# FP4 quantising on 16-bit halves in larger parts, node ranks as sums of signs on ScalarE, six chunks' base products ahead of the tail, takes replanned

## The chip, the cores and the metric

The program runs on one core of a Trainium2 chip. The metric is the device time of one execution in microseconds (us), the median of three runs. Engines are named as in the profile: PE is TensorE (matmul; PEld its weight loads), DVE is VectorE, ACT is ScalarE, POOL is GpSimd, SP is SyncE, which issues most DMA transfers. The engines run their own instruction streams in order and wait for each other through semaphores.

## The reference, cut to what matters

1,250 nodes with 1,024 features, 40,000 edges sorted by their receiver. The output is x plus a graph attention layer plus a mixing layer, and then a feed-forward layer in FP4.

```python
xn = _layernorm(x, axis=-1)
x = x + _L0_gnn_ref(xn, edge_index, ...) + _L0_mix_ref(xn[None], ...)[0]
x = x + _L0_ffn_ref(_layernorm(x, axis=-1)[None], gate_w, up_w, down_w, s_in, s_in_down)[0]

# attention: per edge, message, score, softmax over the edges of a receiver, weighted sum
msg = xl[src] + xr[dst]
act = jnp.where(msg > 0, msg, NEG_SLOPE * msg)
e = jnp.einsum('ehd,hd->eh', act, att)
out = jax.ops.segment_sum(alpha[..., None] * xl[src], dst, num_segments=n)

# feed-forward: weights and rows are rounded to FP4 with a scale for each block of 16
amax = jnp.max(jnp.abs(xb), axis=-1, keepdims=True)
sc8 = jnp.clip(amax / FP4_MAX * global_scale, 0.0, FP8_MAX).astype(jnp.float8_e4m3fn)
q = jnp.sign(xb) * _FP4_VALS[jnp.digitize(a, _FP4_MIDS)]      # 0, .5, 1, 1.5, 2, 3, 4, 6
```

## The kernel before, in words

Nodes lie in 10 chunks of 128. The work has three stages.

**The opening.** x is normalised (`xhat`), turned on PE (`xhat_t`) and multiplied by the small attention weights (groups `hid`, `lr`, `lin`); two tables, `xr_table` and `msg_table`, go to HBM. PE then forms the Gram matrix (`gram`, 16 groups). Meanwhile DVE counts the edges of each node (`one_hots`, `hist`), and ranks the nodes by their count, so that nodes with about as many neighbours share a chunk: `key_row` holds all 1,280 keys in every partition, `key_col` the own ones, and for each chunk one `tensor_scalar` compares the row with the own key and sums (`rank_f`). POOL scatters node, start and degree to their place (`perm_dram`), SP reads them back (`placed`, semaphore `perm_in`), POOL reads the neighbour lists (`neigh`) and the `xr` rows, and DVE makes the indices `idx` from which POOL gathers message rows.
DVE also quantises the three feed-forward weights (n = 0 to 2: gate, up, down). `weight_max(n)` takes the largest of each block of 16, `weight_factors(n)` makes the scales, and `piece(q)` rounds a quarter of a weight: `quantized` on 1,024 columns, from `wslot[n % 2]` to `wq_bf[q % 2]`, with `wt` as scratch. SP stores each piece (`store(q)`); they come back turned in the tail. The rounding works on f32 words: a mask keeps the exponent and sets one bit below it, and adding and subtracting that number rounds the value.

**The rounds.** 62 rounds of 5 or 6 neighbours for each of 128 nodes. In round g, DVE multiplies by `att_sb` (L1626), sums over features (L1628), takes the smallest score (L1633), adds the receiver to the next round's rows (`add_receiver`, L1456) and sums the weighted rows of the round before (`close`, L1464). ACT makes the exponentials (L1081) and the weighted rows (L1094), POOL gathers and rescales.
In the same time PE forms the mixing layer's products: groups `p`, `kv`, `t1`, `t2` (16 each), two `bias` groups, and `base`, two for each of the first EARLY chunks: 1,024 x 1,024 products of `xhat_t` and `mat_a`, 128x512 in f32, 8 matmuls a group. Every group goes to the next of four PSUM banks, and DVE or ACT must take group n - 4 before group n starts. In which round a take stands is planned ahead by a few numbers, not by what PE has done: `PRODUCTS_AT`, `ROUND_0_AT`, `ROUND_STEP`. `sum_p0(n)`, 16 in all, sum weight rows times `colsum` on DVE; eight stand ahead of round 0 and eight in rounds 0 to 3.

```python
at = max(at, freed.get(n - 4, 0))
at += GROUP_STEP.get(kind, 7.0)
round_of[n] = max(0, math.ceil((at - ROUND_0_AT) / ROUND_STEP))
```

**The tail.** The attention comes back from HBM (`gnn_dram`), PE turns it (L894) and adds it by two halves a chunk: `x2(c, h)` (L884), with the base products first where c >= EARLY (L881). The order of these is the table `X2_PLAN`. DVE adds each half (`residual`, L1566), `tail_scales(k)` and `rows_rounded` / `hidden_rounded` call `scales` and `quantized` for 1,024 and 512 columns, PE turns the rows (L903), multiplies by the gate and up weights (L914) and by the down weight (L936). DVE, PE and ACT work on neighbouring chunks in a pipeline of steps k.

## Time and profile before

| | |
|---|---|
| median of three runs | 927.51 us |
| lowest and highest | 926.6 and 928.5 us |
| span of the profiled execution, from its first to its last instruction (no other time of it is given) | 926.9 us, 0.6 below the median |
| busy in it: PE | 858.0 us (93%) |
| DVE | 859.4 us (93%) |
| ACT | 551.4 us (59%) |
| POOL | 471.8 us (51%) |

The profile is of one execution of its own, so sums are made in its 926.9 us. A busy share says nothing of where an engine waits; the views below go by stretches of the span, by groups of instructions, and by instructions in order of time with what ended the idle time ahead of them.

### The profile page before, as it was taken

How to read it: one execution, taken by the hardware profiler on the slowest of the kernel's cores; microseconds unless marked ns; L12 is line 12 of the kernel's file. 1: busy time of each engine (PE TensorE's matmuls, PEld its weight loads, DVE VectorE, ACT ScalarE, POOL GpSimd, SP SyncE). 2: the span in 40 equal slices, each digit the busy share in tenths (PEclk: the TensorE clock that was granted, in tenths of full speed). 3: DMA queues.
4: the chain of work that ended last, by engine and by line, in shares of the span. 5: the costliest groups of instructions: out<-in, count | busy, mean ns of one | idle time of the engine just before them, and what ended most of it. 6: DMA issues, size and time to landing. Idle time of an engine off the chain costs nothing.

```text
span 926.9 us, 9510 instructions
## 1 busy us (share of the span) xinstructions
PE 858.0 (93%) x2724; PEld 419.7 (45%) x2734; DVE 859.4 (93%) x988; ACT 551.4 (59%) x1949; POOL 471.8 (51%) x512
## 2 busy tenths in 40 slices
PE   4999999999999999999999999999999679989664
PEld 3885455644444444444444444444444234444221
DVE  6999989969999999999999999999998599999995
ACT  3313123208687887879998988888888333343422
POOL 5200445376677767777777777877872100010101
PEclk9999999999999999999999999999999798999868
DMA  9322635362385333563345633349830311113124
GB/s 304 97 104 42 149 115 174 111 201 70 80 184 187 95 88 94 190 214 93 100 108 183 193 97 100 100 105 250 317 78 16 104 44 45 69 24 68 26 42 86
DMA packets 64946, 109.97 MB, mean 119 GB/s; under 512 B 29223, under 2 KB 36036, under 8 KB 64874
## 3 DMA queue, kind: packets, MB, share of 16 engines
q0 software_dynamic: 19856, 55.42, 24.0%
q1 hardware_dynamic: 45034, 53.92, 18.3%
q8 instruction: 21, 0.34, 0.2%
q14 instruction: 35, 0.29, 0.1%
HBM read 89.15 MB, written 17.17 MB: 115 GB/s over the span
## 4 chain that ended last, share of the span: by engine, by line
DVE 67%; issue 14%; POOL 10%; DMA 3%; PE 3%; ACT 1%; SPq 0%; DVEq 0%; ACTq 0%; POOLq 0%
DVE z L1628 9%; DVE turned L1456 9%; DVE turned L1626 8%; DVE acc_sb L1464 8%; POOL round_mem L551 7%; DVE round_mem L1210 3%; DVE round_mem L1214 2%; DVE round_mem L1211 2%; DVE round_mem L1209 2%; DVE round_mem L1206 2%; DVE round_mem L1207 2%; DVE round_mem L1208 2%; DVE big_b L1418 1%; DVE big_a L1421 1%; DVE big_b L1566 1%
## 5 line engine op out<-in xcount | busy, mean ns | idle before, releaser
L551 POOL DMA_INDIRECT round_mem<-msg_table,idx x352 | 342.8, 974 | 116.8 <-issue 79.4
L1094 ACT ACTIVATE round_mem<-round_mem,pz 128x65 f32<-128x65 f32 x1408 | 354.4, 398 | 6.9 <-DVE acc_sb L1464 3.0
L726 PE MATMUL acc<-wslot,big_a 128*128 128x512 f32 x512 | 222.3, 597 | 3.1 <-DVE big_b L1418 3.1
L726 PEld LDWEIGHTS acc<-wslot,big_a 128*128 128x128 f32 x512 | 97.8, 192 | 126.0 <-issue 123.8
L1464 DVE TENSOR_REDUCE acc_sb<-round_mem 128x260 f32<-128x1820 f32 (+1 forms) x62 | 121.6, 1962 | 6.5 <-ACT round_mem L1094 4.0
L1081 ACT ACTIVATE pz<-z 128x7 f32<-128x7 f32 (+1 forms) x248 | 55.5, 296 | 106.8 <-DVE z L1633 106.4
L726 PE MATMUL acc<-wslot,big_b 128*128 128x512 f32 x256 | 110.0, 593 | 0.0
L726 PE MATMUL acc<-big_b,wslot 128*128 128x512 f32 x256 | 110.0, 593 | 0.0
L1456 DVE TENSOR_TENSOR turned<-round_mem,turned 128x1560 f32<-128x1560 f32 (+1 forms) x62 | 105.4, 1700 | 2.3 <-DVE z L1633 0.2
L1628 DVE TENSOR_REDUCE z<-turned 128x24 f32<-128x1560 f32 (+1 forms) x62 | 105.1, 1695 | 2.1
L1626 DVE SCALAR_TENSOR_TENSOR turned<-turned,att_sb 128x1536 f32<-128x1536 f32 (+1 forms) x62 | 103.6, 1671 | 0.0
L726 PE MATMUL acc<-big_a,xhat_t 128*128 128x512 f32 x224 | 96.3, 593 | 0.0
L726 PE MATMUL acc<-big_b 128*128 128x512 f32 (+3 forms) x240 | 80.7, 496 | 0.0
L726 PEld LDWEIGHTS acc<-wslot,big_b 128*128 128x128 f32 x256 | 48.7, 190 | 61.1 <-issue 61.1
L726 PEld LDWEIGHTS acc<-big_b,wslot 128*128 128x128 f32 x256 | 48.7, 190 | 61.1 <-issue 61.1
L726 PEld LDWEIGHTS acc<-big_a,xhat_t 128*128 128x128 f32 x224 | 42.6, 190 | 53.5 <-issue 53.2
L671 POOL TENSOR_TENSOR round_mem<-acc_sb,pz 128x260 f32<-128x260 f32 x62 | 47.7, 769 | 33.5 <-DVE acc_sb L1464 29.7
L693 POOL TENSOR_TENSOR rstd<-small,minus_half 128x1 f32<-128x1 f32 x10 | 7.2, 718 | 105.3 <-ACT small L1107 105.3
L726 PEld LDWEIGHTS acc<-big_b 128*128 128x128 f32 x240 | 43.1, 194 | 35.2 <-issue 29.5
L1160 ACT ACTIVATE round_mem<-acc,cscale 128x512 f32<-128x512 f32 x10 | 6.9, 687 | 66.7 <-PE acc L914 66.7
L699 POOL DMA_DIRECT2D out_x<-acc_sb x9 | 8.0, 890 | 72.9 <-ACT acc_sb L1117 69.2
L1024 ACT COPY big_a<-acc 128x512 f32<-128x512 f32 x16 | 9.2, 587 | 58.1 <-PE acc L726 42.6
(222 smaller groups left out, 1043.5 us busy)
## 6 DMA issues: line engine op xcount, KB each, us to landing
big_b<-in_x SPq DMA_DIRECT2D x18, 512.0 KB, 10.4
round_mem<-msg_table,idx POOLq DMA_INDIRECT x352, 2.8
out_x<-big_b SPq DMA_DIRECT2D x9, 512.0 KB, 2.6
out_x<-acc_sb POOLq DMA_DIRECT2D x9, 512.0 KB, 5.5
wslot<-in_wv_t SPq DMA_DIRECT2D x2, 2048.0 KB, 11.5
wslot<-in_wk_t SPq DMA_DIRECT2D x2, 2048.0 KB, 12.5
wslot<-in_wo_t SPq DMA_DIRECT2D x2, 2048.0 KB, 10.0
wslot<-in_wq SPq DMA_DIRECT2D x2, 2048.0 KB, 10.1
```

Of the source, the lines that this page charges most:

```text
L551: pool.indirect_dma_start(xg[g % 4][:, j, :], None, msg_table, bass.IndirectOffsetOnAxis(idx[:, c, j0 + j:j0 + j + 1], 0)).then_inc(xg_in[ ...
L671: nc.gpsimd.tensor_tensor(halves_of[g % 3][:, :, :, n].rearrange("p i (h d) -> p i h d", d=MR), running[c].rearrange("p (i h d) -> p i h d ...
L726: mm = nc.tensor.matmul(o(acc[:, n % 4, :]), a, b, start=first, stop=last)
L1081: ins = nc.scalar.activation(pz[:, g % 2, 0:slots + 1, h], z[:, g % 3, 0:slots + 1, h], ACT.Exp, scale=-1.0, bias=z[:, (g + 1) % 3, top_sl ...
L1094: ins = nc.scalar.activation(to[:, :, j], xg[g % 4][:, j, h * HR + 1:(h + 1) * HR], ACT.Copy, scale=pz[:, g % 2, j, h:h + 1])
L1206: step(nc.vector.tensor_tensor(blocks(v), blocks(v), spread(inv), ALU.mult))
L1207: step(nc.vector.tensor_scalar(t.bitcast(I32), v.bitcast(I32), EXPONENT, HALF_BIT, ALU.bitwise_and, ALU.bitwise_or))
L1210: step(nc.vector.scalar_tensor_tensor(to, v, 6.0 * UP + FP4_MAX, t, ALU.min, ALU.subtract))
L1456: return nc.vector.tensor_tensor(m4[:, 0:n], xg[g % 4][:, 0:n, :].rearrange("p j (h d) -> p j h d", d=HR)[:, :, :, 0:MR], receiver.unsquee ...
L1464: nc.vector.tensor_reduce(running[c].rearrange("p (i f) -> p i f", i=2), halves_of[g % 3][:, :, :, 0:n + 1], AX.X, ALU.add).then_inc(sum_d ...
L1626: step(nc.vector.scalar_tensor_tensor(m4[:, 0:slots, :, 1:MR], m4[:, 0:slots, :, 1:MR], 0.0, att_sb[0:NC].unsqueeze(1).to_broadcast([NC, s ...
L1628: step(nc.vector.tensor_reduce(zz[:, 0:slots, :], m4[:, 0:slots], AX.X, ALU.add))
```

## The change

- `quantized` works on 2,048 columns of a weight at a time (six pieces in place of twelve), and, after the multiply by `inv` in f32, on 16-bit values: a mask takes the upper half of each f32 word and lays the elements of a row out turned (first all first elements of the blocks, then all second ones), and seven further steps are `tensor_scalar` and `tensor_tensor` on bf16. The block scale `sc8` is bf16. The rounded values are written over the slot's own memory (`steps_of`), so the next weight's load into the slot waits for their stores as well (`wt_out`).
- The ranks are made on ACT: the sum of the signs of the differences, one `activation` for each chunk, between and behind the takes of `lr`; DVE turns the sums into ranks (`rank_i`).
- DVE's order in the opening changes with it: the ranks are waited for behind `weight_factors(1)`, ahead of piece 2; only piece 2 stands between them and the wait for `placed`, and pieces 4 and 5 stand behind the indices.
- All 16 `sum_p0` stand in rounds 0 to 7.
- EARLY is 6: chunk 6's base products are made in the tail, in `x2(6, h)`. `ROUND_0_AT` is 168, `X_AT` 55: takes and `add_bias` stand in other rounds.

```diff
-EARLY = 7
+EARLY = 6
...
-HALF_BIT = 0x00400000
-UP = 2.0 ** 22
+CELL, MIDDLE = 0xFFE0, 0x0010
+BINADE, HALF_BIT = 0x7F80, 0x0040
...
-ROUND_0_AT, ROUND_STEP = 196.0, 8.5
+ROUND_0_AT, ROUND_STEP = 168.0, 8.5
 
...
-BIAS_SUMS_AT, X_AT = 40, 54
+BIAS_SUMS_AT, X_AT = 40, 55
...
+        cells = wt.bitcast(BF16)
+        steps_of = [wslot[q // 2 % 2][:, q % 2 * 2 * D:q % 2 * 2 * D + D].bitcast(BF16) for q in range(6)]
...
+                to = gu_dram[q * 2 * P:(q + 1) * 2 * P, :] if q < 4 else dn_dram[(q - 4) * 4 * P:(q - 3) * 4 * P, :]
+                j = 2 if q < 4 else 4
+                sp.dma_start(to.rearrange("(j p) d -> p j d", p=P),
+                             steps_of[q].rearrange("p (j d) -> p j d", j=j)).then_inc(wt_out[q // 2], 16)
...
             sp.wait_ge(w_quantized, 1)
+            sp.wait_ge(wt_out[0], 32)
             sp.dma_start(view(2), uses[2][1]).then_inc(w_in[0], 16)
...
+            def rank(c):
+
+                if c == 0:
+                    act.wait_ge(key_in, 32)
+                nc.scalar.activation(is_above, key_row, ACT.Sign, scale=-1.0, bias=key_col[:, c:c + 1],
+                                     accum_out=rank_f[:, c:c + 1]).then_inc(ranked, 1)
+                act.wait_ge(ranked, c + 1)
+
             for c in range(C):
                 take(index_of["lr", c])
+                if c >= 4:
+                    rank(c - 4)
+            for c in range(6, C):
+                rank(c)
             take(index_of["lin", 0])
...
-                step(nc.vector.tensor_tensor(sc8, sc8, magic, ALU.subtract))
+                step(nc.vector.tensor_tensor(amax, amax, magic, ALU.add))
+                step(nc.vector.tensor_tensor(sc8, amax, magic, ALU.subtract))
...
-                step(nc.vector.tensor_tensor(blocks(v), blocks(v), spread(inv), ALU.mult))
-                step(nc.vector.tensor_scalar(t.bitcast(I32), v.bitcast(I32), EXPONENT, HALF_BIT, ALU.bitwise_and, ALU.bitwise_or))
-                step(nc.vector.tensor_scalar(t, t, 1.5 * UP, 6.0 * UP, ALU.max, ALU.min))
-                step(nc.vector.scalar_tensor_tensor(v, v, 1.0 / UP, t, ALU.mult, ALU.add))
-                step(nc.vector.scalar_tensor_tensor(to, v, 6.0 * UP + FP4_MAX, t, ALU.min, ALU.subtract))
-                return nc.vector.scalar_tensor_tensor(blocks(to), blocks(to), -FP4_MAX, spread(sc8), ALU.max, ALU.mult)
+                nb = width // QB
+                rows_in = v.shape[1] // width
+
+                def turned_blocks(a):
+                    return a.rearrange("p (r i b) -> p r i b", r=rows_in, i=QB)
+
+                high = v.bitcast(U16).rearrange("p (r b i t) -> p r i b t", r=rows_in, i=QB, t=2)[:, :, :, :, 1]
+                by_block = v.rearrange("p (b i) -> p b i", i=QB)
+                step(nc.vector.tensor_tensor(by_block, by_block, inv.unsqueeze(2).to_broadcast([v.shape[0], rows_in * nb, QB]), ALU.mult))
+                step(nc.vector.tensor_scalar(turned_blocks(cell.bitcast(U16)), high, CELL, MIDDLE, ALU.bitwise_and, ALU.bitwise_or))
+                step(nc.vector.tensor_scalar(way.bitcast(U16), cell.bitcast(U16), BINADE, HALF_BIT, ALU.bitwise_and, ALU.bitwise_or))
+                step(nc.vector.tensor_scalar(way, way, 1.5, 64.0, ALU.max, ALU.mult))
+                step(nc.vector.tensor_tensor(cell, cell, way, ALU.add))
+                step(nc.vector.tensor_tensor(way, cell, way, ALU.subtract))
+                step(nc.vector.tensor_scalar(way, way, -FP4_MAX, FP4_MAX, ALU.max, ALU.min))
+                spread = sc8.rearrange("p (r b) -> p r b", r=rows_in).unsqueeze(2).to_broadcast([v.shape[0], rows_in, QB, nb])
+                return nc.vector.tensor_tensor(turned_blocks(to), turned_blocks(way), spread, ALU.mult)
...
-                n, i = divmod(q, 4)
+                n, i = divmod(q, 2)
                 if q >= 1:
                     dve.wait_ge(wq_done, q)
-                if q >= 2:
-                    dve.wait_ge(wt_out[q % 2], 16 * (q // 2))
-                sc8, inv = (f[:, i * 64:(i + 1) * 64] for f in w_factors[n][0:2])
-                quantized(wslot[n % 2][:, i * D:(i + 1) * D], wq_bf[q % 2], (sc8, inv), wt).then_inc(wq_done, 1)
+                inv, sc8 = (f[:, i * 128:(i + 1) * 128] for f in w_factors[n][0:2])
+                quantized(wslot[n % 2][:, i * 2 * D:(i + 1) * 2 * D], steps_of[q], (sc8, inv), cells, steps_of[q],
+                          D if n < 2 else I).then_inc(wq_done, 1)
...
-            piece(0)
             dve.wait_ge(hist_read, PIECES)
             step(nc.vector.tensor_copy(hist, hist_ps))
             step(nc.vector.tensor_tensor_scan(hist_inc, ones32, hist, 0.0, ALU.mult, ALU.add))
             nc.vector.tensor_copy(tot[:], hist_inc[:, DG_LO - 1:DG_LO]).then_inc(tot_done, 1)
             step(nc.vector.tensor_scalar(key, hist, DEG_MAX, KEY_STEP, ALU.min, ALU.mult))
             nc.vector.tensor_tensor(key, key, key_node, ALU.add).then_inc(key_done, 1)
-            piece(1)
+            piece(0)
             step(nc.vector.tensor_tensor(hist_exc, hist_inc, hist, ALU.subtract))
             dve.wait_ge(off_done, 1)
             nc.vector.tensor_scalar(hist_exc, hist_exc, tp[0:DG_HI, 1, 0:1], None, ALU.add).then_inc(csr_done, 1)
             weight_max(1)
-            dve.wait_ge(key_in, 32)
-            for c in range(C):
-                step(nc.vector.tensor_scalar(is_above, key_row, key_col[:, c:c + 1], None, ALU.is_gt, ALU.add,
-                                             accum_out=rank_f[:, c:c + 1]))
-            nc.vector.tensor_copy(rank_i, rank_f).then_inc(rank_done, 1)
-            piece(2)
-            piece(3)
+            piece(1)
             weight_end(0)
             weight_factors(1)
-            piece(4)
+            dve.wait_ge(ranked, C)
+            nc.vector.tensor_scalar(rank_i, rank_f, -0.5, 0.5 * (NP - 1), ALU.mult, ALU.add).then_inc(rank_done, 1)
+            piece(2)
...
-            piece(5)
...
-            piece(6)
-            piece(7)
+            piece(3)
             weight_end(1)
...
-            weight_factors(2)
-            piece(8)
...
-            piece(9)
-            piece(10)
-            piece(11)
+            weight_factors(2)
+            piece(4)
+            piece(5)
             weight_end(2)
...
-            for n in range(KB):
-                sum_p0(n)
...
-                if g < KB // 2:
-                    sum_p0(KB + 2 * g)
-                    sum_p0(KB + 2 * g + 1)
+                if g < KB:
+                    sum_p0(2 * g)
+                    sum_p0(2 * g + 1)
...
-            add_bias(C - 2)
+            for c in range(min(LAST + 1 - X_AT, C - 2), C - 1):
+                add_bias(c)
```

DVE in the opening, between the largest of the second weight and the nodes' flags. Before, from the ranks on (two pieces, factors and a third piece follow them, each piece the six instructions L1206 to L1211):

```order
L1334 TENSOR_SCALAR round_mem<-round_mem 128x1280 [waits key_in]
L1334 TENSOR_SCALAR round_mem<-round_mem 128x1280 [waits dve_step] x9
L1336 CAST round_mem<-round_mem 128x10 [waits dve_step]
L1206 TENSOR_TENSOR wslot<-wslot,round_mem 128x1024 [waits wt_out0,wq_done]
L1207 TENSOR_SCALAR round_mem<-wslot 128x1024 [waits dve_step]
```

Of the changed kernel, from the end of `weight_factors(1)` to the wait for `placed`:

```order
L1347 TENSOR_SCALAR round_mem<-round_mem 128x10 [waits ranked,dve_step]
L1216 TENSOR_TENSOR wslot<-wslot,round_mem 128x2048 [waits wq_done]
L1217 TENSOR_SCALAR round_mem<-wslot 128x2048 [waits dve_step]
L1218 TENSOR_SCALAR wslot<-round_mem 128x2048 [waits dve_step]
L1219 TENSOR_SCALAR wslot<-wslot 128x2048 [waits dve_step]
L1220 TENSOR_TENSOR round_mem<-round_mem,wslot 128x2048 [waits dve_step]
L1221 TENSOR_TENSOR wslot<-round_mem,wslot 128x2048 [waits dve_step]
L1222 TENSOR_SCALAR wslot<-wslot 128x2048 [waits dve_step]
L1224 TENSOR_TENSOR wslot<-wslot,round_mem 128x2048 [waits dve_step]
L1350 TENSOR_TENSOR round_mem<-placed,cap_f 128x10 [waits perm_in]
```

The ten compares are gone from DVE, the wait for ACT's sums (`ranked`) stands there, and one piece is left ahead of the wait for `perm_in`.

DVE at the first round. Before (`big_b` at L1584 and L1587 is the sum of `sum_p0`, L1418 is the take of a `p` group):

```order
L1584 TENSOR_SCALAR big_b<-wslot,colsum 128x512 [waits w_in1,colsum_done,acc_full]
L1587 SCALAR_TENSOR_TENSOR big_b<-wslot,colsum,big_b 128x512 [waits p0_summed] x7
L1454 COPY turned<-xr_sb 128x260 [waits xr_in]
L1456 TENSOR_TENSOR turned<-round_mem,turned 128x1560 [waits xg_in0,dve_step]
L1418 SCALAR_TENSOR_TENSOR big_b<-big_b,colsum,acc 128x512 [waits vb_in,acc_full,dve_step]
L1418 SCALAR_TENSOR_TENSOR big_b<-big_b,colsum,acc 128x512 [waits vb_in,acc_full] x2
L1626 SCALAR_TENSOR_TENSOR turned<-turned,att_sb 128x24x64
```

Of the changed kernel:

```order
L1454 COPY turned<-xr_sb 128x260 [waits xr_in]
L1456 TENSOR_TENSOR turned<-round_mem,turned 128x1560 [waits xg_in0,dve_step]
L1624 SCALAR_TENSOR_TENSOR turned<-turned,att_sb 128x24x64 [waits dve_step]
L1626 TENSOR_REDUCE z<-turned 128x24 [waits dve_step]
L1630 COPY z<-top_first 128x4 [waits dve_step]
L1631 TENSOR_REDUCE z<-z 128x4 [waits dve_step]
L1456 TENSOR_TENSOR turned<-round_mem,turned 128x1560 [waits xg_in1,z_done]
L1584 TENSOR_SCALAR big_b<-wslot,colsum 128x512 [waits colsum_done,w_in1,acc_full,dve_step]
L1587 SCALAR_TENSOR_TENSOR big_b<-wslot,colsum,big_b 128x512 [waits p0_summed]
```

Eight sums and three takes stood ahead of round 0's first product; now they stand two by two in the rounds, and the first take in round 2.

PE in the tail, from the fourth turning of attention to the first turned rows. Before:

```order
L894 MATMUL turned<-ident,acc_sb 128x128 x4
L884 MATMUL acc<-wslot,xr_sb 128x512 x4
L884 MATMUL turned<-wslot,xr_sb 128x512 x2
L894 MATMUL turned<-ident,acc_sb 128x128 x4
L884 MATMUL turned<-wslot,xr_sb 128x512 x4
L903 MATMUL turned<-identb,round_mem 128x128 x8
```

Of the changed kernel:

```order
L893 MATMUL turned<-ident,acc_sb 128x128 x4
L883 MATMUL acc<-wslot,xr_sb 128x512 x4
L880 MATMUL turned<-big_a,xhat_t 128x512 x8
L883 MATMUL turned<-wslot,xr_sb 128x512 x2
L893 MATMUL turned<-ident,acc_sb 128x128 x4
L883 MATMUL turned<-wslot,xr_sb 128x512 x4
L902 MATMUL turned<-identb,round_mem 128x128 x8
```

The eight base products (L880) of `x2(6, 1)` stand ahead of the last two chunks' attention and of the first turned rows; those of `x2(6, 0)` stand two steps later in the same way.

## Rows read from the trace of the kernel before

**Rows 1.** Windows: us, busy us (instructions) per engine, PE clock, DMA share, GB/s

```profile
60.60:187.20 126.60, 126.60 (x459) 72.59 (x456) 117.79 (x149) 34.06 (x90) 43.54 (x42) 0.97 0.45 128
...
204.30:721.00 516.70, 512.68 (x1203) 227.93 (x1201) 501.82 (x414) 429.85 (x1702) 377.21 (x403) 1.00 0.48 133
721.00:927.00 206.00, 154.99 (x546) 70.03 (x556) 178.25 (x313) 69.26 (x120) 16.96 (x20) 0.88 0.23 56
```

**Rows 2.** Timeline of DVE, one piece: start, duration, instruction, count

```profile
55.43 0.16 DVE L1285 RECIPROCAL cscale<-gmax 128x1 f32<-128x1 f32 x1
...
60.60 1.23 DVE L1206 TENSOR_TENSOR wslot<-wslot,round_mem 128x1024 f32<-128x1024 f32 x1
...
66.98 0.17 DVE L1322 COPY round_mem<-turned 40x32 f32<-40x32 f32 x1
```

**Rows 3.** DVE's groups by shape: count, busy us and mean ns, idle before

```profile
L1211 DVE SCALAR_TENSOR_TENSOR round_mem<-round_mem 128x1024 bf16<-128x1024 bf16 x18 | 22.0, 1225 | 0.6
L1334 DVE TENSOR_SCALAR_CACHE_REDUCE round_mem<-round_mem 128x1280 bf16<-128x1280 f32 x10 | 15.4, 1545 | 0.3
...
L1206 DVE TENSOR_TENSOR round_mem<-round_mem 128x1024 f32<-128x1024 f32 x10 | 12.2, 1225 | 0.3
...
L1207 DVE TENSOR_SCALAR round_mem<-round_mem 128x1024 int32<-128x1024 int32 x10 | 7.0, 697 | 0.3
...
L1206 DVE TENSOR_TENSOR round_mem<-round_mem 128x512 f32<-128x512 f32 x10 | 6.9, 686 | 0.1
...
L1261 DVE TENSOR_TENSOR wslot<-round_mem 125x3200 bf16<-125x3200 bf16 x2 | 3.6, 1820 | 0.0
```

**Rows 4.** ACT's groups by shape

```profile
L1105 ACT ACTIVATE round_mem<-big_b,mean_var 128x1024 bf16<-128x1024 f32 x10 | 11.5, 1148 | 0.3
```

**Rows 5.** Timeline of ACT, first half of the take of lr 4

```profile
77.84 0.47 ACT L1009 ACTIVATE acc_sb<-acc,rrms 128x256 f32<-128x256 f32 x1 [0.88 <-PE acc L726]
```

**Rows 6.** Timeline of POOL in the opening

```profile
95.69 1.90 POOL L600 DMA_INDIRECT perm_dram<-round_mem  x1 [15.84 <-DVE round_mem L1336]
...
126.61 1.03 POOL L629 DMA_INDIRECT round_mem<-src_table,start_i  x1 [1.89 <-issue]
...
153.47 0.94 POOL L633 DMA_INDIRECT xr_sb<-xr_table,node_pi  x1 [0.30 <-issue]
```

**Rows 7.** Timeline of SP's queue

```profile
108.81 1.22 SPq L484 DMA_DIRECT2D wslot<-in_down_w  x1
118.54 0.36 SPq L487 DMA_DIRECT2D placed<-perm_dram  x1
```

**Rows 8.** Timeline of DVE, its waits in the opening and round 0

```profile
123.56 0.17 DVE L1343 TENSOR_TENSOR round_mem<-placed,cap_f 128x10 f32<-128x10 f32 x1 [3.21 <-DMA placed<-perm_dram]
...
194.16 0.49 DVE L1584 TENSOR_SCALAR big_b<-wslot,colsum 128x512 f32<-128x512 f32 x1 [6.96 <-issue]
...
204.34 1.76 DVE L1626 SCALAR_TENSOR_TENSOR turned<-turned,att_sb 128x1536 f32<-128x1536 f32 x1
```

**Rows 9.** Timeline of PE, base products and first work of the tail

```profile
622.79 96.30 PE L726 MATMUL acc<-big_a,xhat_t 128*128 128x512 f32 x224
728.15 1.11 PE L894 MATMUL turned<-ident,acc_sb 128*128 128x128 f32 x4 [9.07 <-DMA acc_sb<-gnn_dram]
```

**Rows 10.** Timeline of ACT, exponentials of round 54

```profile
654.45 0.88 ACT L1081 ACTIVATE pz<-z 128x6 f32<-128x6 f32 x4
```

**Rows 11.** Windows of the tail

```profile
728.15:783.15 55.00, 47.53 (x139) 21.68 (x142) 44.66 (x82) 18.83 (x39) 1.73 (x3) 0.88 0.14 55
783.15:864.41 81.26, 74.66 (x269) 33.99 (x272) 77.74 (x134) 31.37 (x55) 7.71 (x9) 0.98 0.21 52
```

**Rows 12.** Timeline of DVE in the tail: chunk 6's second half, one hidden chunk

```profile
785.45 0.69 DVE L1566 SCALAR_TENSOR_TENSOR big_b<-acc,big_b 128x512 f32<-128x512 f32 x1
...
848.62 0.69 DVE L1206 TENSOR_TENSOR round_mem<-round_mem 128x512 f32<-128x512 f32 x1
...
852.33 0.74 DVE L1535 SCALAR_TENSOR_TENSOR round_mem<-acc,cscale,round_mem 128x512 f32<-128x512 f32 x1
```

More of the change, by code:

```diff
@@ L229, in gps_layer @@
         key_done = sem("key_done")
-        rank_done, perm_out, perm_in = sem("rank_done"), sem("perm_out"), sem("perm_in")
+        ranked, rank_done = sem("ranked"), sem("rank_done")
+        perm_out, perm_in = sem("perm_out"), sem("perm_in")
         xr_out, xr_in = sem("xr_out"), sem("xr_in")
@@ L237, in gps_layer @@
         tail_w_in = sem("tail_w_in")
-        wt_out = [sem("wt_out0"), sem("wt_out1")]
+        wt_out = [sem(f"wt_out{n}") for n in range(3)]
         stored = sem("stored")
@@ L291, in gps_layer @@
         qa = tail_mem[0:NC, 3 * D:4 * D]
+        row_cells, row_steps = (qa[:, i * I:(i + 1) * I].bitcast(BF16) for i in range(2))
         x_last = tail_mem[0:LAST_ROWS, 3 * D:4 * D]
@@ L305, in gps_layer @@
         tail_max, tail_g = blocks_of[:, 0], blocks_of[:, 1]
[L306 removed]
+        tail_factors = [(blocks_of[:, 4 + 2 * i, 0:NB // 2].bitcast(BF16), blocks_of[:, 5 + 2 * i]) for i in range(2)]
         gnn_out = [xr_sb[:, c, 0:HID] for c in range(C)]
@@ L471, in _ @@
                 sp.dma_start(unplaced[:, :, 2], csr_dram[1].rearrange("(c p) -> p c", p=NC)).then_inc(csr_in, 16)
-            store(1)
+            store(0)
             sp.wait_ge(csr_done, 1)
@@ L477, in _ @@
                 sp.dma_start(unplaced[:, :, 1], csr_dram[0].rearrange("(c p) -> p c", p=NC)).then_inc(csr_in, 16)
-            store(2)
             sp.wait_ge(acc_taken["act"], taken[index_of["lin", 0]])
@@ L481, in _ @@
             sp.dma_start(msg_table.rearrange("(c p) f -> p c f", p=NC), acc_sb[:]).then_inc(table_out, 16)
-            store(3)
+            store(1)
             sp.wait_ge(w_quantized, 1)
+            sp.wait_ge(wt_out[0], 32)
             sp.dma_start(view(2), uses[2][1]).then_inc(w_in[0], 16)
@@ L487, in _ @@
                 sp.dma_start(placed[:], perm_dram.rearrange("(c p) t -> p c t", p=NC)).then_inc(perm_in, 16)
-            for q in range(4, 8):
+            for q in range(2, 4):
                 store(q)
             sp.wait_ge(w_quantized, 2)
+            sp.wait_ge(wt_out[1], 32)
             sp.dma_start(view(3), uses[3][1]).then_inc(w_in[1], 16)
-            for q in range(8, 11):
-                store(q)
+            store(4)
             sp.wait_ge(acc_full, index_of["gram", 15] + 1)
@@ L496, in _ @@
             sp.dma_start(bk_bc, bk.rearrange("(a d) -> a d", a=1).to_broadcast([P, D])).then_inc(vb_in, 16)
-            store(11)
+            store(5)
             sp.wait_ge(w_quantized, 3)
+            sp.wait_ge(wt_out[2], 32)
             sp.dma_start(view(4), uses[4][1]).then_inc(w_in[0], 16)
@@ L508, in _ @@
             sp.wait_ge(acc_full, read_by[10])
-            sp.wait_ge(wt_out[0], 16 * 6)
-            sp.wait_ge(wt_out[1], 16 * 6)
+            for n in range(3):
+                sp.wait_ge(wt_out[n], 32)
             for k in range(4):
@@ L1192, in scales @@
                 if g.shape[1] == 1:
[L1193 to L1211 removed]
+                    return nc.vector.tensor_scalar(inv, magic, g, TIE_UP, ALU.mult, ALU.mult)
@@ new lines, in scales, with quantized @@
+                return nc.vector.scalar_tensor_tensor(inv, magic, TIE_UP, g, ALU.mult, ALU.mult)
+            def quantized(v, to, factors, cell, way, width):
+                sc8, inv = factors
+                nb = width // QB
[13 more added lines that the diff above has]
+                return nc.vector.tensor_tensor(turned_blocks(to), turned_blocks(way), spread, ALU.mult)
@@ L1557, in hidden_rounded @@
                 sc8, inv = tail_factors[(c + 1) % 2]
-                quantized(hidden, h_bf[c % 2], (sc8[:, D // QB:], inv[:, D // QB:]), qa[:, 0:I]).then_inc(h_done, 1)
+                quantized(hidden, h_bf[c % 2], (sc8[:, D // QB:], inv[:, D // QB:]), row_cells[:, 0:I], row_steps[:, 0:I], I).then_inc(h_done, 1)
             def residual(c, h):
@@ L1601, in add_base @@
                 step(nc.vector.tensor_tensor(b, base_at[c], b, ALU.add))
-            assert round_of[index_of["bias", 1]] < X_AT <= LAST - (C - 3)
+            assert round_of[index_of["bias", 1]] < X_AT
             def sum_bias(k):
```

50 lines of the change are left out of this document (13 added, 37 removed).

## The prediction

> **What bounds the kernel now.** First the busy shares by stage, then who waits in each. In the opening (60.6 to 187.2) VectorE (DVE) is busy 117.8 of 126.6 us and TensorE (PE) all of it; in the 62 rounds DVE is busy 501.8 and PE 512.7 of 516.7 us; in the tail DVE 178.3 and PE 155.0 of 206 us [rows 1]. PE is not waited for in the rounds: it runs the products ahead of DVE and must only be done when the tail starts. It ends the base products at 622.79 + 96.30 = 719.1 and then stands idle 9.1 us for the attention that comes back from HBM at 728.2 [rows 9]. So DVE's order of work sets the start of the rounds and their end, and PE is some 9 us short of being the bound there. In the opening DVE waits only twice, 3.2 us for the sorted nodes (`placed`) at 123.6 and 7.0 us at 194.2, behind the branch over the skipped overflow block [rows 8]. The first product of round 0 (the multiply by `att`) starts at 204.34.
>
> **One piece.** A piece is six instructions on 1,024 columns, 60.60 to 66.98, 6.4 us [rows 2], so 12.8 for 2,048. The new one has eight on 2,048. The rows give the rates: two-source f32 686 ns for 512 columns and 1,225 for 1,024, so 0.15 + 1.05 ns per element; two-source all in 16 bits 1,820 ns for 3,200, so 0.15 + 0.52; one-source 32-bit, the int32 mask included, 697 for 1,024, so 0.15 + 0.52; `scalar_tensor_tensor` gains nothing from bf16, 1,225 for 1,024 [rows 3]. Then:
> - the f32 multiply by `inv`: 2.29 us.
> - the three `tensor_tensor` in bf16: 0.15 + 2,048 x 0.52 = 1.22 each, 3.66.
> - the three one-source operations in 16 bits: no row has one. Above they cost the 32-bit row's 1.22 each. Two bytes in place of four double the two-source rate [rows 3]; the same factor gives 0.15 + 2,048 x 0.26 = 0.69. I take 0.69, 2.07 for three. The Trainium skill, VectorE: DVE Perf Modes, section The perf-mode tier table, gives 693 ns for such an operation on 2,048 bf16 elements; by it the sum stays as it is, and no run here shows it yet.
> - the mask that reads the upper halves, 64 bytes apart, and writes them turned: no row has such a stride. Its nearest rows are the same mask on neighbouring words, 0.52 ns an element (1.22), and the two-source f32 row, 1.05 (2.29). I take the middle, 1.76: the stride may cost the rate that the mask has now, or nothing, and no row tells.
>
> Sum 9.78, and 0.2 for the gaps of 0.03 to 0.04 between dependent instructions: **10.0 us**, bounds 9.4 to 12.1. Six pieces: 60 us in place of 77.
>
> **The opening.** The ten compares of the ranks leave DVE, 15.4 us [rows 3], 16 with reading each sum. On ScalarE (ACT) one costs 1.15 us for 1,024 elements with an accumulator [rows 4], so with a quarter more elements and the reading of the sum about 1.5. Six of them sit behind the takes of lr 4 to 9, each 0.85 us [rows 5]: from 78.7 on ACT goes 2.35 per chunk, to 91.9, and four more end at **97.9**. PE is not held: it has four banks, and its next groups (`lin` and the first gram groups) need only lr 6 to 9 taken, done by 90.6 while PE is still at the first of them. DVE meanwhile: it starts the ranks now at 95.3 - 16 = 79.3, with two pieces behind it. Without these 12.8 us, with pieces 0 and 1 (20.0), the factors of the second weight that now stand ahead of the wait (5.2 by 55.43 to 60.60 [rows 2], and 0.3 to end the first) and 1.2 because the histogram has no piece in front of it any more, it comes there at 93.2 and waits 4.7 us. The ranks are done 2.6 us later than now, so the ten scatters on GpSimd (POOL) start at 98.3 and not 95.7 and end at 112 [rows 6].
> Their data took until 118.5 to be seen by SyncE, beside the 2-MB weight load issued at 108.8, and `placed` landed at 123.5 [rows 7, 8]. Now that load waits for the store of piece 1, which queues behind the two table writes, to about 115; the scatters thus meet less traffic. I set this against the 2.6 us: `placed` at **124**, 119 to 130. Behind this wait stand on DVE the starts of all neighbour lists, and POOL's neighbour reads (126.6 now) wait for them. DVE has only piece 2 to do ahead of it (done at 108.1), so 15 us of the saving turn into a longer wait.
> From the wait to 187.2 DVE now needs 63.6 us with seven pieces (44.8), so 18.8 of other work. After: 124 + 18.8 + 3 x 10.0 + 0.6 for the third weight, that lands about 126 = **173.4**. POOL is no later: its neighbour and xr reads run 126.6 to 154.4 [rows 6] and keep their distance to `placed`; the first gather can then start at 155, and all lists are ready before that. Then the 7.0 us behind the branch stay. Of the 17.1 us from 187.2 to 204.34 the first eight column sums (5.9) and three takes (2.1) go into the rounds, 9.2 stay: round 0's first product at 182.6, **21.7 earlier**.
>
> **The rounds.** The 5.9 and 2.1 come back inside them, and one `add_bias` of 1.2 moves behind them: 21.7 - 5.9 - 2.1 + 1.2 = **14.9 earlier** at their end; the attention is back at 728.2 - 14.9 = 713.3. PE: two base groups of 96.30 / 14 = 6.9 us are gone, 705 if nothing held it. But takes stand in later rounds (the last t2 take in round 54, was 51). PE can be four groups ahead of them; it starts the second base group when round 54's take is done, near 654.4 - 13.7 = 640.7 [rows 10], and 11 groups end at 716.4. That is 3 us behind the attention, paid for by the first tail products, which come at full clock and not after a gap of 9 us (granted clock 0.88 in that stretch, against 0.98 after) [rows 11]. I count 0.
>
> **The tail.** PE gets chunk 6's base products, 2 x 6.9 = 13.8 us, the first half ahead of the first turned rows. In its first 55 us PE is busy 47.5 [rows 11]: with 13.8 more it needs 61.3, some 4 less at full clock (0.88 is granted now). Of its 7.5 idle us there I let it fill 2 (the rest are waits for ACT and DVE at fixed places): chunk 6's second half is ready 13.8 - 4 - 2 = 7.8 later. PE has it now at 783.1, DVE adds it at 785.4 [rows 12], 2.3 later: so DVE stands 5.5 us later from there. After that DVE is the longer of the two, 77.7 of 81.3 us busy against PE's 74.7. A row chunk (1,024) saves by the same rates 6.38 - 5.7 = 0.7, a hidden chunk (512) 848.62 to 852.33 = 3.7 - 3.55 = 0.15 [rows 12]: 0.85 in each of 7 to 8 steps, 6.4 in all. Added base and bias sums even out. Tail: 5.5 - 6.4 = **-0.9**, near nothing.
>
> Sum: 14.9 + 0.9 = 15.8 off the span of 926.9, rounded down to 15.5 for the steps where PE is as long: 911.4. The median of the runs is 0.6 above that span: **912.0 us**, 1.7% faster.
>
> **Rivals.**
> - *The strided mask is slow (slower).* Its place: piece 3 to 5 and each tail chunk. If each element cost two cycles (2.08 ns, twice the one-a-cycle row) a piece grows by 2.65, the three by 8, a tail step by 2.0, nine of them by 18: 938 us. It decides from 0.78 + 0.76 = about 1.55 ns an element. For it: nothing in the trace reads with such a stride. Against it: the int32 mask has two elements a cycle to give away. Chance 0.12. A rule of the Trainium skill speaks for it: Vector Engine (DVE) Microarchitecture Reference, section 5.2 Measured stream behaviour, says a stream that hops at every element takes 1.7 to 2.5 ns per element in place of 1.05. At 2.5 ns the same sum gives 948; no run here shows it.
> - *The 16-bit one-source operations run like the 32-bit ones.* A piece is 11.6, a tail step 1.2 longer: 4.8 + 10 on top, 927, no change. Chance 0.06.
> - *The chain of the ranks or PE takes the gain.* `placed` at 130 and not 124 puts all 6 us onto the start; or PE's 13.8 us in the tail are not absorbed. 918 to 925. For it: DVE waits there already; PE is busy 99% of the rounds. Chance 0.17.
> - *More than that.* The mask at two a cycle (0.5 us per piece and tail chunk, 3 to 4 us in all) and a shorter stop behind the branch, which now coincides with a 2-MB load: 900 to 906. Chance 0.2.
>
> The forecast's own case, 906 to 918, has 0.45. Within 0.2% (1.9 us, about what three runs can tell from no change) lie the second rival and edges of the first and third, 0.05; slower 0.13; faster 0.82. Range 902 to 926.
>
> **What would show it.** Right: eight instructions a piece, 9.4 to 10.5 us; a wait of 12 to 18 us at `perm_in`; the `att` product of round 0 near 183; rounds ending about 15 us earlier; PE's idle gap ahead of the tail gone; the tail as long as now, with DVE waiting for PE around chunk 6. Wrong: a mask above 3 us for 2,048; takes that wait in the rounds for PE; `placed` later than 130; a tail longer by more than 5 us.

## The result and the profile after

The changed kernel took 937.8 us (median; 935.1 to 942.2), the kernel before 927.1 beside it: ratio 1.0122, 95% interval 1.0101 to 1.0144. The forecast was 912.0. The profiled execution has a span of 935.0 us, clock 0.968. One execution in this document is left out of the ratios: 5,109 us, one of the ten of e10.

VectorE's groups in the opening (out<-in, shapes, count | busy us, mean ns of one | idle before):

```profile
L1217 DVE TENSOR_SCALAR round_mem<-wslot 128x2048 uint16<-128x2048 uint16 x6 | 11.8, 1968 | 0.2
L1216 DVE TENSOR_TENSOR wslot<-wslot,round_mem 128x2048 f32<-128x2048 f32 x4 | 9.2, 2296 | 0.0
...
L1220 DVE TENSOR_TENSOR round_mem<-round_mem,wslot 128x2048 bf16<-128x2048 bf16 x6 | 7.3, 1225 | 0.2
...
L1218 DVE TENSOR_SCALAR wslot<-round_mem 128x2048 uint16<-128x2048 uint16 x6 | 4.2, 694 | 0.2
```

The costs of a piece came close to the forecast: 2.30 + 1.97 + 3 x 0.69 + 3 x 1.22 = 10.0 us busy for 2,048 columns, where 9.78 was forecast; with the gaps between its eight instructions piece 3 lasts 10.3 us (132.42 to 142.72), where 10.0 was forecast. So the slowdown is not in the quantising. VectorE's timeline of the opening (start, duration, engine line op, [idle before it <- what ended it]):

```profile
97.61 0.17 DVE L1347 TENSOR_SCALAR round_mem<-round_mem 128x10 int32<-128x10 f32 x1 [3.39 <-ACT round_mem L1057]
...
125.57 0.17 DVE L1350 TENSOR_TENSOR round_mem<-placed,cap_f 128x10 f32<-128x10 f32 x1 [17.66 <-DMA placed<-perm_dram]
...
182.99 0.43 DVE L1454 COPY turned<-xr_sb 128x260 f32<-128x260 f32 x1 [5.41 <-issue]
...
185.28 1.76 DVE L1624 SCALAR_TENSOR_TENSOR turned<-turned,att_sb 128x1536 f32<-128x1536 f32 x1
...
192.88 1.79 DVE L1456 TENSOR_TENSOR turned<-round_mem,turned 128x1560 f32<-128x1560 f32 x1 [3.32 <-DMA round_mem<-msg_table,idx]
```

These answer to [rows 8]. Round 0 starts at 185.28, 19.1 us earlier than before. Then the lead melts. The start of the multiply by `att` (L1626 before, L1624 after), read from the two timelines round by round:

| round | before | after | lead | what took it |
|---|---|---|---|---|
| 0 | 204.34 | 185.28 | 19.1 | |
| 1 | 212.06 | 195.89 | 16.2 | 3.3 waited for gather(1) |
| 4 | 242.65 | 225.76 | 16.9 | |
| 8 | 276.46 | 266.51 | 10.0 | the column sums, now in the rounds to 7 |
| 28 | 442.58 | 435.04 | 7.5 | takes that stood earlier before |
| 41 | 541.11 | 536.88 | 4.2 | 3.5 waited for the last t1 take |
| 55 | 658.25 | 652.79 | 5.5 | |
| 56 | 666.75 | 670.34 | -3.6 | 9.0 waited for x |

Two lines of VectorE's timeline stand behind the last two losses, and two of SyncE's queue behind the second:

```profile
536.21 0.75 DVE L1610 TENSOR_SCALAR big_b<-big_b,bq_col 128x1024 f32<-128x1024 f32 x1 [3.54 <-ACT big_b L1026]
...
669.20 1.23 DVE L1594 TENSOR_TENSOR big_b<-big_b 128x1024 f32<-128x1024 f32 x1 [8.96 <-DMA big_b<-in_x]
```

```profile
644.53 14.41 SPq L516 DMA_TRANSPOSE wslot<-gu_dram  x8
658.99 0.58 SPq L517 DMA_DIRECT2D wslot<-in_w_up  x1
659.61 4.96 SPq L520 DMA_DIRECT2D big_b<-in_x  x9
```

x is loaded behind twelve transposed weight loads, and these wait for the end of t2 on TensorE: 638.8 now, 621.3 before. Why was TensorE 17.6 us late with a VectorE that was early? Its timeline:

```profile
205.86 8.80 PE L725 MATMUL acc<-wslot,big_a 128*128 128x512 f32 x16 [3.15 <-DVE big_b L1421]
...
265.98 20.87 PE L725 MATMUL acc<-wslot,big_a 128*128 128x512 f32 x48 [2.84 <-DVE big_b L1421]
292.18 17.01 PE L725 MATMUL acc<-wslot,big_a 128*128 128x512 f32 x32 [3.65 <-DVE big_b L1421]
...
689.49 21.05 PE L725 MATMUL acc<-big_a,xhat_t 128*128 128x512 f32 x43 [6.24 <-ACT xhat_t L1030]
```

Six such waits for takes, 14.4 us in all, lie between 205 and 292 (before: two, 3.1 us). The windows of 180 to 300, before and then after (columns as in [rows 1]):

```profile
180.00:300.00 120.00, 116.86 (x280) 52.45 (x279) 110.55 (x105) 70.17 (x284) 82.57 (x86) 0.99 0.54 146
```

```profile
180.00:300.00 120.00, 105.58 (x240) 46.09 (x239) 111.29 (x96) 79.26 (x321) 88.58 (x94) 0.94 0.50 130
```

40 products fewer were done by 300: at 96.30 / 224 = 0.43 us each [rows 9] that is 17.2 us (an estimate, but the end of t2 is late by the same 17.6). 11.3 of them are the busy time that is missing; the rest fits the granted clock, 0.94 and not 0.99.

The tail: the first transpose of the attention starts at 733.13 (728.15 before), right behind the last base product and 10.65 us behind the last round's closing sum (9.26 before). From there to the end are 201.9 us (198.75). Windows from 733.1, answering to [rows 11]:

```profile
733.10:788.10 55.00, 49.96 (x155) 23.20 (x156) 41.09 (x86) 19.44 (x41) 1.73 (x3) 0.97 0.12 46
788.10:869.40 81.30, 76.64 (x269) 34.94 (x273) 70.89 (x148) 30.69 (x53) 6.11 (x8) 1.00 0.21 52
```

TensorE and VectorE have changed places: 76.6 busy against 70.9, before 74.7 against 77.7.

### The profile page after: what moved, and what is told of

It is laid out like the page before. It is cut to its first block, busy times and chain, and to the rows that moved or that the text cites. A ratio compares the mean times of both kernels' runs of the same rounds, so it can differ in the third digit from the quotient of the medians.

```text
span 935.0 us, 9515 instructions
## 1 busy us (share of the span) xinstructions
PE 862.1 (92%) x2724; PEld 420.4 (45%) x2734; DVE 820.0 (88%) x983; ACT 564.0 (60%) x1967; POOL 485.4 (52%) x512
## 4 chain that ended last, share of the span: by engine, by line
PE 57%; DVE 21%; issue 7%; POOL 6%; DMA 3%; SPq 2%; ACT 2%; ACTq 0%; POOLq 0%; DVEq 0%
PE acc L725 46%; PE turned L880 2%; DVE turned L1456 2%; DVE z L1626 2%; DVE acc_sb L1464 2%; DVE turned L1624 2%; POOL round_mem L553 2%; SPq L516 2%; PE acc L880 1%; PE acc L883 1%; PE acc L913 1%; POOL round_mem L631 1%; POOL perm_dram L602 1%; DMA big_b<-in_x 1%; PE turned L935 1%
## 5 line engine op out<-in xcount | busy, mean ns | idle before, releaser
L725 PE MATMUL acc<-wslot,big_a 128*128 128x512 f32 x512 | 228.0, 607 | 14.4 <-DVE big_b L1421 14.4
L1626 DVE TENSOR_REDUCE z<-turned 128x24 f32<-128x1560 f32 (+1 forms) x62 | 105.1, 1695 | 2.1
L1624 DVE SCALAR_TENSOR_TENSOR turned<-turned,att_sb 128x1536 f32<-128x1536 f32 (+1 forms) x62 | 103.5, 1670 | 0.0
L725 PE MATMUL acc<-big_a,xhat_t 128*128 128x512 f32 x192 | 85.4, 606 | 7.5 <-ACT xhat_t L1030 6.2
L725 PEld LDWEIGHTS acc<-big_a,xhat_t 128*128 128x128 f32 x192 | 37.3, 195 | 55.5 <-issue 46.1
L698 POOL DMA_DIRECT2D out_x<-acc_sb x9 | 8.3, 926 | 72.0 <-ACT acc_sb L1125 67.4
## 6 DMA issues: line engine op xcount, KB each, us to landing
wslot<-in_wq SPq DMA_DIRECT2D x2, 2048.0 KB, 10.1
```

The lines of the kernel that those rows point to most:

```text
L725: mm = nc.tensor.matmul(o(acc[:, n % 4, :]), a, b, start=first, stop=last)
L1624: step(nc.vector.scalar_tensor_tensor(m4[:, 0:slots, :, 1:MR], m4[:, 0:slots, :, 1:MR], 0.0, att_sb[0:NC].unsqueeze(1).to_broadcast([NC, s ...
L1626: step(nc.vector.tensor_reduce(zz[:, 0:slots, :], m4[:, 0:slots], AX.X, ALU.add))
```

## The experiments

Theory A: the planner puts round 0 at 168, and it is really at 185; takes come 17 us too late for TensorE's four banks, its lateness makes x late, and that stops VectorE. Theory B: VectorE's own added work in the rounds is the cost.

**e1, the plan.**

```diff
-ROUND_0_AT, ROUND_STEP = 168.0, 8.5
+ROUND_0_AT, ROUND_STEP = 180.0, 8.5
```

> The changed kernel with one number altered, ROUND_0_AT = 180 in place of 168, so that the planner's round 0 stands 5 us ahead of where it was measured (185.3) and not 17. Theory A (the takes are planned too late for the products): TensorE's waits for the bias-adding takes in 180 to 300 fall from 14.4 us to under 4, the granted clock there is back at 0.98 or more, the products of t2 end near 622 and not 638.8, the loads of x are issued near 644 and not 659.6, and VectorE's wait of 9.0 us for them shrinks to under 3: 919 to 926 us. Theory B (the column sums and takes that moved into the rounds cost VectorE the time, TensorE only follows): the waits may go, but the rounds end where they did, 724.5, and the time stays within 2 us of 937.

926.5 us, ratio to the kernel before 0.9999 (0.9983 to 1.0016): one number gives back the whole loss, so theory B, which had the time within 2 us of 937, falls. The wait of 3.5 at 536 is gone, the transposed loads go out at 628.0 and not 638.8. But not all waits went. TensorE's timeline:

```profile
265.03 7.13 PE L725 MATMUL acc<-wslot,big_a 128*128 128x512 f32 x16 [1.62 <-DVE big_b L1421]
...
282.54 7.66 PE L725 MATMUL acc<-wslot,big_a 128*128 128x512 f32 x13 [7.01 <-DVE big_b L1421]
```

With one of 1.45 between these two they sum to 10.1 us, so the expected "under 4 us" was missed, and with it the clock (0.96, expected 0.98 or more), the end of t2 (629.5, expected 622) and the wait for x (5.3, expected under 3). The cause: rounds 1 to 8 last 10 us, with two column sums each, and the planner counts 8.5. Round 10 stands in the plan at 180 + 85 = 265 and is at 283.1, 18 us late; before it was 294.3 against 281, 13 late, and in the changed kernel 284.0 against 253, 31 late. The waits for takes follow in the same order: 3.1 us with 13, 10.1 with 18, 14.4 with 31. VectorE still waits 5.28 us for x.

**e2, the order on SyncE.**

```diff
-            (the twelve transposed loads and w_up)
             sp.wait_ge(acc_full, index_of["bias", 1] + 1)
             for c in range(C - 1):
                 sp.dma_start(base[:, c, :], x[c * NC:(c + 1) * NC, :]).then_inc(x_in[c], 16)
+            (the twelve transposed loads and w_up)
```

> The changed kernel with the nine loads of x issued ahead of the twelve transposed weight loads on SyncE and not behind them; the plan of takes stays late. Theory A: the products are as late as before (t2 ends at 638.8), but x lands near 650 and not 669, so VectorE's wait of 9.0 us and TensorE's of 6.2 us behind it go; the rounds end near 715.5; TensorE's last base product ends near 723, the tail starts there: 924 to 929 us. Theory C (the transposed loads are what matters, and become late for the tail): a new wait in the tail, no gain, 935 us or more.

928.1 us, 1.0002 (0.9987 to 1.0016). The plan is still late, TensorE's waits for takes up to 292 are nearly the same (13.2 us), the loads of x go out at 640.15 in place of 659.61, and the 9.0 us on VectorE and the 6.2 on TensorE are gone; the tail starts at 724.1, 9.0 earlier. Theory C falls: the transposed loads are issued from 645 to 683, in the changed kernel from 639 to 659, and the tail is as long (202.2 us against 201.9).

**e3, both.**

> Both edits: ROUND_0_AT = 180 and the loads of x ahead of the transposed weights. Theory A: both causes gone, the rounds end 9 to 15 us earlier than 724.5 and the attention decides the tail's start again, 716 to 723; 914 to 922 us. Theory B: not under 930 us.

921.0 us, 0.9940 (0.9924 to 0.9957), as expected of theory A. TensorE's row ahead of the tail shows that the attention sets the start again, at 717.1:

```profile
717.14 0.66 PE L893 MATMUL turned<-ident,acc_sb 128*128 128x128 f32 x4 [3.80 <-DMA acc_sb<-gnn_dram]
```

**e4, what the strided mask costs.** Six masks in VectorE's wait at `placed`, in the order of the expectation:

```diff
+            step(nc.vector.tensor_scalar(out_of, hop, CELL, MIDDLE, ALU.bitwise_and, ALU.bitwise_or))
+            step(nc.vector.tensor_scalar(po, pu[:, 0:2 * D], CELL, MIDDLE, ALU.bitwise_and, ALU.bitwise_or))
+            step(nc.vector.tensor_scalar(po, near, CELL, MIDDLE, ALU.bitwise_and, ALU.bitwise_or))
...
```

> The changed kernel with six more masks of 2,048 or 1,024 elements on VectorE behind piece 2, where it waits 17.7 us for the sorted nodes; their results are not used. In their order: the upper halves 64 bytes apart, turned, as the kernel has it (1.97 us expected again); 16-bit neighbours (0.69); the upper halves of neighbouring words, 4 bytes apart (1.22 if a 16-bit element in every 32-bit word runs like a 32-bit one; 1.97 if the packing of halves alone costs the time); 16-bit elements 32 bytes apart (1.97 if any far hop costs 0.89 ns; 0.69 if only the read width counts); 1,024 words 64 bytes apart (0.69 at the neighbouring word's rate, 1.06 at 0.89 ns per hop); 1,024 neighbouring words (0.69). The time of the whole stays within 3 us of the changed kernel's.

```profile
107.50 1.97 DVE L1359 TENSOR_SCALAR round_mem<-wslot 128x2048 uint16<-128x2048 uint16 x1
109.51 0.69 DVE L1360 TENSOR_SCALAR round_mem<-wslot 128x2048 uint16<-128x2048 uint16 x1
110.24 1.23 DVE L1361 TENSOR_SCALAR round_mem<-wslot 128x2048 uint16<-128x2048 uint16 x1
111.50 2.05 DVE L1362 TENSOR_SCALAR round_mem<-wslot 128x2048 uint16<-128x2048 uint16 x1
113.58 1.04 DVE L1363 TENSOR_SCALAR round_mem<-wslot 128x1024 int32<-128x1024 int32 x1
114.65 0.69 DVE L1364 TENSOR_SCALAR round_mem<-wslot 128x1024 int32<-128x1024 int32 x1
```

Less 0.15 us to start: neighbours in 16 bits 0.26 ns an element, every second half (4 bytes apart) 0.53, neighbouring words 0.53, any far hop 0.87 to 0.93, for 16-bit elements 32 or 64 bytes apart and for words alike. What costs is the hop, not the width of the element. All three far hops read in the turned order and write neighbours, so hop and turned order are one thing here. The time stayed at 939.0 us in one run: six masks (7.9 us) in a wait cost nothing that one run can show.

**e5, the plan again**: e3 with ROUND_0_AT = 186.

> As the run with both edits, but ROUND_0_AT = 186. With 180 TensorE still waited 9.8 us for takes between 265 and 284, because rounds 1 to 8, which now hold the column sums, last 10 us and not the planner's 8.5. Theory A: those waits fall under 4 us and the last base product ends 6 us or more earlier; the attention (717.1) already set the tail's start, so TensorE's wait ahead of the tail grows from 3.8 to about 9 and the time stays, 919 to 923 us. Against it: if TensorE's lateness still counted somewhere in the rounds, under 918 us.

923.6 us, 0.9965 (0.9949 to 0.9981), just above the expected 919 to 923. TensorE's waits shrink to 2.9 us at 273, it is done with the base products 12.3 us ahead of the attention, and nothing comes of it:

```profile
715.77 1.11 PE L893 MATMUL turned<-ident,acc_sb 128*128 128x128 f32 x4 [12.29 <-DMA acc_sb<-gnn_dram]
```

The tail starts 1.4 us earlier than in e3 and lasts 1.9 longer, 203.1 against 201.3: after the idle 12.3 us its first 55 us run at a granted clock of 0.88 (0.94 in e3 behind 3.8 us, 0.97 in the changed kernel, which has no such gap).

**e6, chunk 6 back ahead of the tail**: e5 with

```diff
-EARLY = 6
+EARLY = 7
```

> The run with ROUND_0_AT = 186 and the loads of x first, and EARLY = 7: chunk 6's base products (13.8 us of TensorE) are back ahead of the tail. Theory: with the takes on time TensorE has some 9 us to spare ahead of the tail, so the tail starts at most 5 us later, and the tail is the old one less VectorE's savings: chunk 6's step stands 5 us earlier in it. Tail 196 to 199 us in place of 201.3; 916 to 921 us. Rival: the 13.8 us are paid in full ahead of the tail, 923 to 926.

912.0 us, 0.9848 (0.9818 to 0.9879), better than the expected 916 to 921 and clear of e5's interval. The idle 12.3 us are filled, the tail starts at 719.5, 3.7 later, and lasts 188.6 us, 14.5 shorter. Windows of its first stretches:

```profile
719.50:774.50 55.00, 48.50 (x160) 22.59 (x163) 48.13 (x100) 22.41 (x45) 2.33 (x4) 1.00 0.17 65
774.50:855.80 81.30, 70.64 (x266) 32.07 (x270) 76.82 (x160) 31.60 (x54) 7.42 (x9) 0.97 0.24 52
```

VectorE is the longer one again, clock 1.00 from the start.

**e7, the ranks back on VectorE**: e5 with the ten compares ahead of piece 1.

```diff
+            dve.wait_ge(key_in, 32)
+            for c in range(C):
+                step(nc.vector.tensor_scalar(is_above, key_row, key_col[:, c:c + 1], None, ALU.is_gt, ALU.add,
+                                             accum_out=rank_f[:, c:c + 1]))
+            nc.vector.tensor_copy(rank_i, rank_f).then_inc(rank_done, 1)
             piece(1)
```

> The run with ROUND_0_AT = 186 and the loads of x first, with the ten compares of the ranks back on VectorE ahead of piece 1. Theory D: VectorE waits 3.4 and 17.7 us ahead of the sorted nodes, so 16 us of compares fit there; the ranks are done at 95.3 and not 97.5, the nodes are back 0 to 2 us earlier, and the time is the same or up to 2 us shorter. Rival (as the prediction counted them): the compares' time comes off VectorE's path, so that they cost 5 us or more.

923.9 us, 0.9972 (0.9955 to 0.9989); e5 has 923.6. Theory D stands: 16 us of VectorE's work taken away or put back make no difference to the time. (In the two profiled executions e7's tail starts 3.6 us later and is 1.6 us shorter.) Its timeline:

```profile
122.06 0.17 DVE L1341 TENSOR_TENSOR round_mem<-placed,cap_f 128x10 f32<-128x10 f32 x1 [1.58 <-DMA placed<-perm_dram]
...
191.30 1.79 DVE L1447 TENSOR_TENSOR turned<-round_mem,turned 128x1560 f32<-128x1560 f32 x1 [4.06 <-DMA round_mem<-msg_table,idx]
```

`placed` is 2.5 us earlier than in e5 (124.6), yet round 1 still waits for gather(1) to 191.3 (190.8): GpSimd starts that gather behind its branch, in which it stands 7.2 us (7.7 in e5).

**e8, column sums in the wait for gather(1)**: e5 with

```diff
+                if g == 0:
+                    for n in range(4):
+                        sum_p0(n)
                 if g < LAST:
                     step(add_receiver(g + 1))
...
-                if g < KB:
-                    sum_p0(2 * g)
-                    sum_p0(2 * g + 1)
+                if 1 <= g < KB - 1:
+                    sum_p0(2 * g + 2)
+                    sum_p0(2 * g + 3)
```

> The run with ROUND_0_AT = 186 and the loads of x first, with four of the sixteen column sums in round 0 ahead of the wait for gather(1) and two in each of rounds 1 to 6. Theory: VectorE waits about 3 us there for GpSimd's gather, and 3.0 us of sums fit into that wait: round 7 starts 2 to 3 us earlier, and so does the tail; 2 to 3 us faster than that run. Rival: the sums' own inputs are not there yet, no gain.

920.7 us, 0.9932 (0.9908 to 0.9955), about 3 us under e5, but the intervals overlap and the profiled tail starts at 716.6, no earlier than e5's. The wait for gather(1) is gone; that this is the gain is not shown.

**e9, EARLY = 7 alone in the changed kernel** (the edit of e6, nothing else).

> The changed kernel with EARLY = 7 and nothing else; the takes stay planned for 168 and x behind the transposed loads. Theory: TensorE is the late one ahead of the tail there (its last base product ends at 733.1, the attention is back near 731.8), so the 13.8 us of chunk 6 push the tail's start to 745 to 747; the tail itself is the 188.6 us of the run with EARLY = 7; 933 to 937 us, no better than the changed kernel's 937.8. Rival (the number of early chunks alone made the change slow): 925 to 928 us.

942.0 us, 1.0159 (1.0125 to 1.0194). The theory had 933 to 937 and a start of the tail at 745 to 747; its direction is right, its size too small, and the rival (925 to 928) falls: x comes another 2.4 us later (11.4 waited), the tail starts at 749.7 behind TensorE and lasts 189.2. VectorE stands at its start:

```profile
753.53 0.69 DVE L1566 SCALAR_TENSOR_TENSOR big_b<-turned,big_b 128x512 f32<-128x512 f32 x1 [17.29 <-PE turned L883]
```

With a late plan chunk 6 is paid ahead of the tail, with fewer early chunks inside it.

**e10, EARLY = 8 in the kernel before.**

> The kernel before with EARLY = 8 and nothing else: chunk 7's base products too stand ahead of the tail, in the 9.1 us that TensorE waits there. Theory E (in the first third of the tail TensorE is what is waited for, and the idle time ahead of it costs clock): the tail starts near 733, 4.8 us later than at 728.15, and is 8 to 13 us shorter than 198.8: 919 to 924 us. Rival (VectorE is the longer of the two in the tail, 77.7 of 81.3 us busy, as the prediction read it): the tail keeps at least 195 us, 927 to 932 us.

931.2 us, 1.0044 (1.0027 to 1.0060). Theory E falls here, the rival is right: the tail starts at 731.2 and lasts 196.8, only 1.9 less. In the old tail VectorE is the longer one (76.9 busy of 81 us from 786, TensorE 67.4), and products taken off TensorE bring little. The filled gap is seen at its front: the first scaling of a hidden chunk (L1535) stands 37.9 us behind the tail's start, 41.1 before; but the nine steps from there to the last take 140.1 us, 138.8 before. So the 188.6 of e6 are not the filled gap alone.

**e11, all together**: e8's sums, with EARLY = 7.

> ROUND_0_AT = 186, the loads of x first, EARLY = 7, and four column sums in round 0 ahead of the wait for gather(1). With EARLY = 7 TensorE works without a gap from 284 to the tail and its last base product ends where the attention is back (719.5), so the sums' 2 to 3 us are hidden behind TensorE: 910 to 912.5 us. Rival: they come off as in the run with EARLY = 6, 908 to 909.5.

909.3 us, 0.9810 (0.9777 to 0.9842), the fastest, 1.9% under the kernel before. The tail starts at 717.1 and lasts 189.7. The rival is nearer (908 to 909.5; the theory had 910 to 912.5): in the profile the tail starts 2.5 us earlier than e6's, so TensorE was not so tight that this could not come through. The intervals of e6 and e11 overlap, so the 2.7 us between their medians are not shown to be real.

## Why the prediction was wrong

**One piece: right.** 10.0 us forecast with its gaps, 10.3 measured. The mask took 1.97 and not 1.76, the f32 multiply 2.30, the one-source operations 0.694. Behind the mask there are six steps on 16 bits, not seven as the text ahead of the prediction has it; the sum has six. The Trainium skill, VectorE: DVE Perf Modes, section The perf-mode tier table, has 693 ns for the one-source operation, and the trace agrees. The 1.7 to 2.5 ns of the Trainium skill, Vector Engine (DVE) Microarchitecture Reference, section 5.2 Measured stream behaviour, stand there in rows of two-source operations on 32-bit words; the one-source mask here took 0.89 ns an element, so the prediction leaned on another case. The strided mask, the slower rival, was priced at 938, which is near the measured time, but that is chance and not the mechanism: it took 0.2 us a piece more than counted. (At 2.5 ns its sum gives 946 and not 948.)

**The opening: right within 2.7 us.** Ranks done at 97.6 (97.9), `placed` at 125.6 (124), a wait of 17.7 (about 16), round 0 at 185.3 (182.6). Two things were missing from it: a wait of 3.7 us for the neighbour lists, and gather(1). "POOL is no later" failed: its first gather starts at 161.2 and not at 155, its branch ends at 180.3, and VectorE gets gather(1) at 192.9, so 2.9 us of the lead go at once. And e7 shows that the ranks' move saves nothing: they leave an engine that waits for their result.

**The rounds: wrong, and this is the step.** "PE is not waited for in the rounds: it [...] must only be done when the tail starts" failed. TensorE was itself made to wait for takes (14.4 us), t2 ended 17.6 us later, x with it, and VectorE waited 9.0 us for x; so the last round starts 3.6 us later than before, where the forecast had it 14.9 earlier. The forecast moved the last round 14.9 us forward by VectorE's sum alone, and said of TensorE "705 if nothing held it", then looked only at the last takes. It never set the planned times against the measured rounds at the first ones. The plan has round 0 at 168, my own forecast 182.6; with rounds that the moved sums stretch to 10 us the takes are 31 us behind the plan at round 10, where they were 13. The first take stands at 205.0; before, three stood at 202.4. So the takes hardly moved at all, though VectorE did. Of the 18.5 us between forecast and measured end of the rounds, 9.0 are the wait for x, which falls to 5.3 with the plan (e1) and goes with the order of the loads (e2), 3.5 the wait for the last t1 take, which goes with the plan (e1), 2.9 gather(1), 2.7 the later start, the rest the sums and takes, about 8.4 in place of 8.0. The sums themselves were priced well; theory B falls with e1. With both edits (e3) the last round starts at 697.3, 10.9 us earlier than before, and the time is 9.0 us above the forecast.

The link over SyncE was not seen either: x waits for t2's end and then behind some 20 us of transposed loads.

**The tail: the shape right, one size wrong.** Forecast +5.5 for chunk 6 and -6.4 for the savings, -0.9 in all; measured +3.1. The ten scalings of hidden chunks (L1535) stand, counted from the tail's start, at 41.1, 57.9 and so on to 179.8 before, at 42.2, 62.9 and so on to 181.1 now. They are 5.0 us later from the second on, near the 5.5 of the forecast; ahead of it VectorE waits for chunk 6's second half.

```profile
795.45 0.69 DVE L1566 SCALAR_TENSOR_TENSOR big_b<-acc,big_b 128x512 f32<-128x512 f32 x1 [4.53 <-PE acc L883]
...
926.86 1.28 DVE L1571 SCALAR_TENSOR_TENSOR big_b<-turned,cscale,big_b 128x1024 f32<-128x1024 f32 x1 [5.11 <-PE turned L935]
```

Up to the last scaling VectorE regains 3.7 and not 6.4, as TensorE with 76.6 of 81.3 us leaves it little room, and behind it 1.8 go again, as the last wait for TensorE grows from 3.1 to 5.1: 5.0 - 3.7 + 1.8 = 3.1. In e6 and in e9, where chunk 6's products are out of the tail, the nine steps from the first to the last scaling take 132.4 us, against 138.8 before: the savings are there, 6.4 us (6.4 forecast).

What was sized wrong is the net of chunk 6. Taken out of the changed kernel's tail it shortens it by 12.7 of its 13.8 us (e9; 14.5 from e5 to e6), and 5.5 were counted. The prediction set "4 of clock" and "2 idle" against it, which were room in the old tail. But TensorE busy up to the tail has a gain of its own: in e9 and e10, without a gap and with chunk 6 ahead, the first scaling stands 37.9 us behind the tail's start and not 41.1. So 12.7 - 3.1 - 6.4 = 3.2, where 3.1 are measured from the kernel before to the changed one. In the old kernel the same 3.2 us at the front came through as 1.9 only (e10).

So the change carries two gains, an earlier start and a cheaper tail step, and was spoilt by numbers beside them: the planned start of the rounds, the order of the loads of x, and one early chunk too few. Not settled: how much of e8's 3 us is the filled wait, since the profiles differ by as much in the opening.
